# Cross attention: products of values in six bursts of two tiles per pair of heads in place of three bursts of four or five tiles

## What is computed

```python
q = _split_heads(x @ qw + qb)
k = _split_heads(ctx @ kw + kb)
v = _split_heads(ctx @ vw + vb)
scores = jnp.einsum('bqhd,bkhd->bhqk', q, k) / np.sqrt(D // H).astype(np.float32)
if mask is not None:
    scores = scores + mask
probs = jax.nn.softmax(scores, axis=-1)
out = jnp.einsum('bhqk,bkhd->bqhd', probs, v)
```

## Time and profile before

| | us |
|---|---|
| median of 3 runs | 1386.95 |
| lowest and highest | 1381.2, 1392.85 |
| the profiled execution, its own time | 1371.47 |
| its span, first to last instruction | 1369.5 |

### The profile page before, as it was taken

How to read it: one execution, slowest core, us unless ns; L and a number is a source line. 1 busy time by engine, 2 the same in 40 slices (tenths; PEclk the granted TensorE clock), 3 DMA queues, 4 the chain that set the end, 5 groups by cost and what they waited for, 6 DMA issues and landing times. The chain is left out here.

```text
span 1369.5 us, 33504 instructions
## 1 busy us (share of the span) xinstructions
PE 1145.1 (84%) x12100; PEld 622.8 (45%) x12100; DVE 1016.8 (74%) x2788; ACT 889.0 (65%) x1789; POOL 362.4 (26%) x796
## 2 busy tenths in 40 slices
PE   5499995699999999999999999985488868859994
PEld 2244444244444444444444444433244435438883
DVE  7478866578888887888988888855699953655665
ACT  4288883187777877778777788781287834534553
POOL 4211113132040411405022040003222222115662
PEclk9599997599999999999999999997699988968997
DMA  5970005513222132211323122000760002311113
GB/s 128 224 150 29 3 2 130 132 54 89 83 62 62 32 98 77 70 54 42 94 68 81 47 45 71 15 2 5 164 116 2 3 1 93 93 35 36 48 47 112
DMA packets 76442, 92.33 MB, mean 67 GB/s; under 512 B 8255, under 2 KB 62503, under 8 KB 76280
## 3 DMA queue, kind: packets, MB, share of 16 engines
q1 hardware_dynamic: 73016, 84.68, 24.6%
q0 software_dynamic: 2496, 5.12, 1.4%
q10 hardware_dynamic: 768, 0.40, 0.1%
HBM read 64.37 MB, written 27.02 MB: 67 GB/s over the span
## 5 line engine op out<-in xcount | busy, mean ns | idle before, releaser
L1450 DVE TENSOR_REDUCE MG<-bank 128x1 f32<-128x401 f32 (+1 forms) x1024 | 514.2, 565 | 76.2 <-PE bank L1234 75.9
L1370 ACT ACTIVATE PT<-bank 128x512 f32<-128x512 f32 (+1 forms) x624 | 334.0, 598 | 75.2 <-PE bank L1252 70.1
L1234 PE MATMUL bank<-KP,QP 54*128 54x401 bf16 (+1 forms) x1024 | 259.6, 346 | 21.5 <-DVE MG L1450 10.7
L1252 PE MATMUL bank<-QP,KP 54*128 54x256 bf16 (+1 forms) x1664 | 268.4, 275 | 5.4 <-ACT QP L1378 1.8
L1272 PE MATMUL bank<-PT,VP 128*9 128x256 f32 (+1 forms) x2688 | 199.2, 369 | 0.8 <-ACT XT L1370 0.8
L1525 POOL TENSOR_TENSOR MP<-MN,ZERO 128x4 bf16<-128x4 f32 x128 | 26.4, 206 | 494.4 <-DVE MN L1457 489.4
L1252 PEld LDWEIGHTS bank<-QP,KP 54*128 54x128 bf16 (+1 forms) x1664 | 116.0, 96 | 78.0 <-PE bank L1252 17.3
L1234 PEld LDWEIGHTS bank<-KP,QP 54*128 54x128 bf16 x1024 | 75.6, 95 | 158.2 <-DVE MG L1450 103.4
L1370 ACT ACTIVATE XT<-bank 128x512 f32<-128x512 f32 (+1 forms) x208 | 116.3, 598 | 39.6 <-PE bank L1252 38.3
L891 PE MATMUL bank<-QP,KP 51*128 51x256 bf16 x512 | 95.3, 280 | 36.4 <-DVE MN L992 8.9
L858 PE MATMUL bank<-KP,QP 51*128 51x256 bf16 x512 | 99.1, 291 | 28.3 <-PEq L113 19.1
(11 more groups left out here) (278 smaller groups left out, 2001.4 us busy)
## 6 DMA issues: line engine op xcount, KB each, us to landing
KP<-ctx_k_parts SPq DMA_DIRECT2D x128, 100.1 KB
ctx_k_parts<-KPARTS SPq DMA_DIRECT2D x16, 600.4 KB, 6.0
KP<-ctx_k_parts SPq DMA_DIRECT2D x128, 59.4 KB
CN<-in_ctx SPq DMA_DIRECT2D x8, 768.0 KB
QP<-q_parts SPq DMA_DIRECT2D x22, 192.0 KB
RAW<-in_w_gate_up SPq DMA_DIRECT2D x8, 512.0 KB, 3.9
ctx_k_parts<-KPARTS SPq DMA_DIRECT2D x16, 200.1 KB, 5.7
q_parts<-parts SPq DMA_DIRECT2D x16, 192.0 KB, 4.6
```

The source lines that it names most:

```text
L1234: nc.tensor.matmul(GRAIN[n % NG][:, 0:w], k.QP[half, p, b * S + 128 * qt:b * S + 128 * (qt + 1)], k.KP[half, p, a:a + w], start=True, stop ...
L1252: return nc.tensor.matmul(bank[0:rows[t], S * at:S * (at + 1)], k.KP[half, p, 128 * t:128 * t + rows[t]], k.QP[half, p, b * S:(b + 1) * S] ...
L1370: nc.scalar.activation(PT[n % NP][0:rows[t], :], bank_of("s", g, t)[0:rows[t], :], ACT.Exp).then_inc(exp_done, 1)
L1450: nc.vector.tensor_reduce(MG[:, g % 4, 2 * s + qt, chunk:chunk + 1], GRAIN[n % NG][:, 0:w], AX.X, ALU.max).then_inc(m_read, 1)
```

## The change

The products of values stand in six bursts: tiles 0 and 1 in step 1, 2 and 3 in step 3, and so on to 8 and 9 in step 9, and tiles 10 to 12 in step 12. The places of "c" and "m" in the list are written as steps 3 and 7, which is where they stood.

```diff
-V_BURSTS = (range(0, 4), range(4, 8), range(8, NTILES))
+V_BURSTS = tuple(range(t, t + 2) for t in range(0, 10, 2)) + (range(10, NTILES),)
...
         if j in bursts:
-            if bursts[j] == 0 and p == 0:
+            if j == 3 and p == 0:
                 plan.append(("c", 0, 0))
-            if bursts[j] == 1:
+            if j == 7:
                 plan.append(("m", 0, 1))
             plan.append(("v", bursts[j], 0))
```

## The result

The changed kernel took 1395.76 us (median of 20 runs, 1387.69 to 1402.8) where the kernel before took 1385.49 us in the same measurement (20 runs, 1380.26 to 1392.85). The ratio is 1.0068, 95% interval 1.0048 to 1.0087: about 9 us slower. I had forecast 12 us faster.

The account below looks back on a forecast made before the run. No engine was full; burst length held each pair, with TensorE, VectorE and ScalarE waiting in a ring. Terms -12.6 - 3.2 + 2.8 + 1.2 = -11.8, rounded to -12, gave 1375 us from the median 1386.95; range 1358 to 1400.

Parts of the forecast that it names:

- The plain pairs: 21 cross attention pairs with no preparation for the next batch: 8.70 to 8.10 us, 0.60 saved each, 12.6 in all.
- The fifth burst: In a plain pair: starts 5.70 us behind the first score and delays exponential 0 of the next pair by 0.2.
- the moved wait: First burst must wait for the previous pair's copy, seen 0.06 us after its end, so it starts at 0.62, not 0.48.
- A burst's price: TensorE's boundary around a burst: 0.10 us leaving, 0.08 entering, 0.31 with lost overlap; about 0.55 from burst to next grain.
- T and K pairs: 21 pairs preparing the next batch's T or K pieces: 0.15 of 10.1 us saved each, 3.2 in all, bounds 0 and 0.4.
- part of the last burst's 0.44: In T and K pairs, ScalarE gives back part of the last burst's 0.44 us shortening, against scores 9 and 10 delayed 0.5.
- V pairs: 14 pairs with value products, delayed 0.46 us by a burst ahead: first +0.05, second +0.35, 2.8 lost in all.
- The first pairs: Eight batch-opening pairs: head sums delayed 0.4 us, shorter last burst returns 0.25, so 0.15 lost each, 1.2 in all.
- a lower clock: Sign of being wrong: granted clock behind the division lower than that stretch has now; no size given.
- Rival 2: TensorE becomes the bound in the 43 prepared pairs: +21 us, 1408; decides from 0.29 a prepared pair; chance 0.17.
- Rival 1: Everything gets smoother: the 43 prepared pairs also gain 0.4 us each, -30 in all, 1357 us; chance 0.15.
- Rival 3: The gain is passed on: copy loop or in-order scores hold plain pairs at 8.5 us; 1387 us; chance 0.18.

Follow-up runs that it names:

- first_only: Against the kernel before, only the first burst split, in all pairs: tiles 0 and 1 in step 1, 2 and 3 in step 3; ratio 1.0046.
- last_only: Against the kernel before, only the last burst split, in all pairs: tiles 8 and 9 in step 9, 10 to 12 in step 12; ratio 0.9930.
- mid_only: Against the kernel before, only the middle burst split, in all pairs: tiles 4 and 5 in step 5, 6 and 7 in step 7; ratio 1.0049.
- after_fill2: Changed kernel plus 16 unread matmuls ahead of the wait of the grain that waits for the division, in seven first pairs; ratio to before 0.9988.
- before_fill: Kernel before plus 16 unread matmuls ahead of the wait of the grain that waits for the division, in seven first pairs; ratio to before 0.9997.
- plain_only: Against the kernel before, six bursts at the new places in pairs 6 and 7 of each batch, joined at the old places elsewhere; ratio 0.9932.
- p0_only: Against the kernel before, the new burst places in pair 0 of each batch alone, the old ones elsewhere; ratio 1.0022.
- p0_fill: New places in pair 0 alone, plus 16 matmuls mistakenly behind the grain's wait, disturbing the output, in first pairs but batch 0's; ratio to before 1.026.
- after_c1: Changed kernel with the head sums in step 1 instead of step 3 of pair 0, nothing else; ratio to before 0.9903.
- mix_c1: Against before: new steps in pairs 0, 1, 6, 7, last burst alone split in 2 to 5, head sums in step 1 of pair 0; 1343.59 us, ratio 0.9842.

## Why the prediction was wrong, point by point

**The plain pairs** went as worked out, with a smaller size. Forecast 8.10, measured 8.26; 21 pairs gave 11.2 us instead of 12.6. At 0.44 each it would be 9.2; the rest came in the last two pairs of the stage, and about 1 us of it because the kernel before ran its very last pair partly at the lower clock (a granted 0.61 from 923.5 to 926.9). TensorE and VectorE in a plain pair:

```profile
606.78 0.27 PE L1252 MATMUL bank<-QP,KP 54*128 54x256 bf16 x1
...
612.63 0.62 PE L1272 MATMUL bank<-PT,VP 128*9 128x256 f32 x8
613.18 0.35 PE L1234 MATMUL bank<-KP,QP 54*128 54x401 bf16 x2
```

```profile
608.15 8.14 DVE L1450 TENSOR_REDUCE MG<-bank 128x1 f32<-128x401 f32 x16
```

The fifth burst stands at 5.85 behind the first score where I had put it at 5.70. VectorE makes 16 reductions in one row; the stop of 0.35 at the eighth is gone, as forecast. Fifteen pitches of 0.48 and a reduction of 0.57 are 7.8, so 0.3 us of shorter stops and lost overlaps are left in the row's 8.14. The step that was off is the moved wait: the copy ends at 606.97 + 0.39 = 607.36 and the first burst starts at 607.51, 0.15 later, not 0.06 (the row 607.51 above names the copy as what it waited for). So the first burst stands at 0.73 instead of 0.62, and 0.11 of the 0.16 is there from the first burst on. Whether the added 0.09 is the copy's signal or the price of entering a burst (0.08 by the prediction) the rows do not separate.

**A burst's price** held: 0.55 from burst to grain (607.51 to 608.06, 612.63 to 613.18).

**T and K pairs.** T pairs gave the 0.16 I had taken (0.15). For the K pairs the sum had a gain of 0.15, and they lost 0.12 and 0.19. The step that failed is the delay of the scores of tiles 9 and 10 against "part of the last burst's 0.44": the middle split alone costs 0.34, the last one alone brings only 0.08. The burst that delays them is the third, in step 5; the fourth, which the prediction names, stands behind them.

**V pairs.** Forecast +0.05 and +0.35, measured +0.18 and +0.63, 5.7 us instead of 2.8. The mechanism was right, to 0.01 us for the first split alone (0.46 in the first V pair). What I over-rated there is what the end of the pair gives back (0.28 instead of 0.41; the last split alone brings 0.24), and what I didn't price is the middle split in the second V pair, 0.36.

**The first pairs** are the step that turned the sign. I had put a delay of 0.4 against 0.25 given back, 0.15 a pair and 1.2 us in all. The delay was right (0.36, and 0.40 in first_only). The shorter last burst gives back 0.07, not 0.25 (last_only), and the middle split, which I had put at nothing, costs 0.36 by itself (mid_only). All three splits together cost 0.52 a pair at the full clock, less than the 0.69 that they cost one by one. The first pair of all, which has no division and runs at the lower clock for most of its length in every kernel, took 15.4 us from its first score where it had taken 13.7; I had not priced it apart. And I took the granted clock of 0.99 for the changed kernel too, naming a lower clock only among what would make me wrong: the longer wait was priced as 0.4 us of time and the clock behind it at nothing.

The terms from the profiles, in us. The third column has the low clock in it, the fourth compares the two kernels with the fill, where there is none between the first and the last copy:

| pairs | forecast | changed against before | after_fill2 against before_fill |
|---|---|---|---|
| 21 plain | -12.6 | -11.2 | -10.2 |
| 7 T and 14 K | -3.2 | -1.1 + 2.2 | -1.1 + 2.2 |
| 14 V | +2.8 | +5.7 | +5.6 |
| 7 first pairs with a division | +1.2 with the next line | +5.1 | +2.5 |
| the first pair of all | | +2.0 | +1.8 (from its first score) |
| the T pair in the long low stretch | 0 | +5.3 | 0 |
| sum | -11.8 | +8.0 | +0.8 |

The third column's +8.0 stands against 7.8 between the two last copies. So the miss has two parts of like size. At the full clock the splits are dearer than I had them in K, V and first pairs and bring less in plain ones, and the gain of 12 is gone; the lower clock behind the longer wait then makes the loss. The fourth column measures the first part; for the second the profiles give some 7 us and the ratios 11.

**The rivals.** Rival 2 had the right sign and the wrong place. T, K and V pairs cost 2.2 + 5.7 - 1.1 = 6.8 us in 35 pairs, 0.19 each and under the 0.29 from which it was to decide; over all its 43 pairs it is 0.45 in the profiled execution and 0.26 by the fourth column, so only the low clock brought it clearly over that. What holds these pairs is not TensorE's added work all along: in K pairs it is ScalarE behind a displaced score, in V pairs VectorE behind displaced values. Rival 1 fell: only the T pairs got shorter. Rival 3 fell in plain_only, with 8.26 where it needed 8.5.

## What to carry to other kernels

When a long piece is cut in two, ask of each half what it stands ahead of now. A half that moves ahead of another engine's input delays that input by its length less what TensorE waited there anyway (0.45 of 0.75 us ahead of the values, 0.36 ahead of the head sums), and the order shows that before anything runs. And where a wait of TensorE of one to two microseconds grows, price the clock behind it as well as the wait. Splits that are good in one kind of iteration are worth a table by kind: here each pair's time depended on its own steps and, by up to 0.16 us, on those of the pair ahead (first pairs of plain_only, T pairs of p0_only).

## What the runs showed of the hardware

In these traces the lower clock behind a wait is a matter of chance, and it came more often behind the longer wait. Each trace has seven first pairs with a division: behind a wait of 1.47 us, 16 of 49 fell to it (seven kernels, from one of seven to five of seven); behind 1.90 us, 14 of 21 (changed, p0_only, first_only), and all seven of p0_fill, with its added work behind the wait; behind 0.56 to 0.58 us, 1 of 14 (after_c1 none, mix_c1 one); where the fill left a wait of 0.15 us or less, none of 21. So a wait of 0.6 us is rarely followed by it here, but not never. One trace of each kernel is a small sample, and p0_only's took 6 us more than that kernel's median. Sixteen matmuls whose result nobody reads were enough to keep it away in all 21. In the six batches of the table a fall cost 0.7 to 1.5 us in most first pairs and 2.4 to 2.7 in four of the 25. Why one low stretch of the changed kernel lasted 20.5 us, over a T pair with no such wait in it, stays open: nothing as long came behind a first pair in the other traces.
